# Routed rows kept as planes of 16-bit halves and loaded by a transposing DMA, with eight result buffers and new instruction orders

## What is computed

```python
h = _layernorm(x) * (1 + ca) + sa
x = x + ga * attn(h)      # h + 0.5 * (mamba forward + mamba backward), 16 states, 512 inner channels
h = _layernorm(x) * (1 + cb) + sb
x = x + gb * ffn(h)       # routed experts plus a shared expert
```

```python
scores = softmax(xt @ gate_w.T); top_vals, idx = top_k(scores, 2)
xs = xt[:, None, :] * weights[:, :, None]
for e in range(8):
    h  = silu(xs @ w1[e].T + b1[e])
    x2 = h @ w2[e].T + b2[e]
    x3 = xs @ w3[e].T + b3[e]
    y  = y + sum(x2 * x3 * mask)
z = (silu(xt @ sw1.T) * (xt @ sw2.T)) @ sw3.T
return y + z
```

## Time and profile before

| | |
|---|---|
| median of 3 runs | 2058.6 us |
| the profiled execution's own time | 2058.04 us |
| its span | 2056.2 us |
| mean granted TensorE clock | 0.922 |
| busy: TensorE, VectorE, ScalarE, GpSimd | 88%, 94%, 78%, 87% |

### The profile page before, as it was taken

One profiled execution on the slowest core, in us unless ns is written; L12 is line 12 of the kernel. 1 busy time (PEld: TensorE's weight loads), 2 busy tenths in 40 slices (PEclk: granted clock), 3 DMA queues, 4 the chain that ended last, 5 costly groups with the idle time before them and its releaser, 6 DMA issues.

```text
span 2056.2 us, 25386 instructions
## 1 busy us (share of the span) xinstructions
PE 1813.9 (88%) x6768; PEld 829.7 (40%) x6768; DVE 1925.5 (94%) x1820; ACT 1599.3 (78%) x3362; POOL 1798.3 (87%) x612
## 2 busy tenths in 40 slices
PE   7788898979898979788898889898977799999997
PEld 3333333424242423232323233332322256569996
DVE  7999999999999999999999999999999998857776
ACT  5886779898989898877788898989896844546664
POOL 5689999999999999999999999999999953545555
PEclk9999898989898989898989989898987899999999
DMA  7736454544545353535362635354545334635555
GB/s 268 244 117 152 105 138 110 134 108 121 124 116 125 109 133 105 124 106 143 85 164 72 157 92 141 100 131 115 131 97 146 112 126 140 253 135 91 94 94 76
DMA packets 140653, 263.93 MB, mean 128 GB/s; under 512 B 21840, under 2 KB 44368, under 8 KB 139488
## 3 DMA queue, kind: packets, MB, share of 16 engines
q1 hardware_dynamic: 125920, 240.58, 43.3%
q0 software_dynamic: 13296, 17.80, 5.0%
q10 hardware_dynamic: 1296, 3.93, 0.5%
HBM read 193.10 MB, written 70.19 MB: 128 GB/s over the span
## 4 chain that ended last, share of the span: by engine, by line
PE 27%; ACT 23%; DVE 22%; issue 16%; POOL 11%; DMA 1%; DVEq 0%; ACTq 0%; POOLq 0%; SPq 0%
DVE hst L1935 13%; ACT psum L1399 9%; POOL hst L1058 7%; DVE dbu L1914 5%; PE psum L2739 4%; PE psum L2495 3%; PE psum L2925 3%; ACT dbu L1431 3%; PE psum L2934 3%; PE psum L2945 3%; PE psum L2753 2%; POOL dbu L1046 2%; PE psum L2415 2%; ACT sp_tmp L1368 1%; ACT dt L1363 1%
## 5 line engine op out<-in xcount | busy, mean ns | idle before, releaser
L1058 POOL TENSOR_TENSOR hst<-hst,c_rep 128x2048 f32<-128x2048 f32 x254 | 1146.8, 4548 | 3.5 <-ACT state L1385 3.4
L1399 ACT ACTIVATE psum<-dt_rep,neg_a 128x512 f32<-128x512 f32 (+1 forms) x1024 | 659.8, 676 | 123.1 <-DVE hst L1935 118.5
L1935 DVE TENSOR_TENSOR_SCAN hst<-psum,state,dbu 128x1024 f32<-128x1024 f32 x264 | 603.8, 2325 | 0.5 <-DVE score L2012 0.4
L1935 DVE TENSOR_TENSOR_SCAN hst<-psum,dbu 128x1024 f32<-128x1024 f32 x248 | 554.6, 2269 | 6.9 <-ACT psum L1399 6.8
L1914 DVE TENSOR_TENSOR dbu<-psum,b_rep 128x2048 f32<-128x2048 f32 x177 | 400.2, 2261 | 6.6 <-PE psum L2480 6.5
L1046 POOL TENSOR_TENSOR dbu<-dtu_rep,b_rep 128x2048 f32<-128x2048 f32 x79 | 360.1, 4559 | 12.4 <-DVE hst L1935 7.4
L2480 PE MATMUL psum<-dt,same 32*128 32x512 f32 x354 | 217.5, 696 | 103.0 <-DVE dbu L1914 94.9
L2495 PE MATMUL psum<-hst,same 128*32 128x512 f32 x2048 | 267.3, 669 | 43.2 <-POOL hst L1058 43.2
L2427 PE MATMUL psum<-xp,taps 128*128 128x512 f32 x512 | 237.1, 606 | 5.4 <-ACT sp_tmp L1365 5.3
L1189 POOL DMA_INDIRECT out_x<-h,target_u x71 | 110.8, 1560 | 107.1 <-issue 51.7
L1431 ACT ACTIVATE dbu<-first_decay,dbu,state 128x1 f32<-128x1 f32 x504 | 160.0, 376 | 20.5 <-DVE dbu L1914 18.9
(11 more groups left out here) (246 smaller groups left out, 2623.9 us busy)
## 6 DMA issues: line engine op xcount, KB each, us to landing
dt_rep<-dt_scratch SPq DMA_DIRECT2D x256, 256.0 KB, 4.8
dtu_rep<-dtu_scratch SPq DMA_DIRECT2D x316, 64.0 KB, 1.9
taps<-taps_scratch SPq DMA_DIRECT2D x64, 256.0 KB, 4.5
b_rep<-bc_scratch SPq DMA_DIRECT2D x64, 256.0 KB, 4.9
c_rep<-bc_scratch SPq DMA_DIRECT2D x64, 256.0 KB, 7.7
dt_scratch<-dt SPq DMA_DIRECT2D x48, 256.0 KB, 6.2
h<-slot_scratch SPq DMA_DIRECT2D x71, 129.5 KB, 2.3
sp_tmp<-t_scratch SPq DMA_DIRECT2D x16, 512.0 KB, 6.9
```

The source lines that it names most:

```text
L1058: nc.gpsimd.tensor_tensor(h, h, c_rep[q % 2][:], ALU.mult).then_inc(prod_done, 1)
L1399: nc.scalar.activation(psum[:, PS_A + i, kept], dt_rep[:, G % 2, j, kept], ACT.Exp, scale=neg_a[:, q % 2, u, i:i + 1]).then_inc(exp_done, 1)
L1935: nc.vector.tensor_tensor_scan(both(hst[:, U % RING, groups, :]), both(psum[:, PS_A + 2 * pair:PS_A + 2 * pair + 2, :]), both(dbu[:, U % D ...
```

## The change

- A routed row is stored in HBM as two planes of 16-bit halves: the 256 low halves of its float32 values, then the 256 high halves, then number and flags, padded to 1088 bytes. ScalarE scales into a new tile `weighed` first, and one more activation copy for each send (2048 elements of 16 bits a partition) parts the halves into `send`.
- In the tile loop SP issues a transposing DMA of 128 rows by 512 halves into `turned_halves` (4 buffers) and a second small DMA of number and flags into `xt_meta` (8 buffers). `turn_tile` is gone from TensorE. `join_halves` on ScalarE takes the place of `copy_tile`: 512 elements of 16 bits from SBUF instead of 256 float32 from PSUM, two tiles ahead instead of one, into 4 buffers.
- The load of tile s+4 waits for `join_halves(s)`, and for the tile s-4 to have been gated.
- The result `yt` has 8 buffers, so `bias_result(s)` waits for the DMA of tile s-8.
- The order lists of TensorE, VectorE and ScalarE behind the scan are new.

```diff
-ROW = DM + 1 + BATCH
+META = 1 + BATCH
+ROW = DM + 16
...
-        target_u = sb3("target_u", [P, IDS], U32)
+        target_u = sb3("target_u", [P, 16], U32)
...
-        yt = part(8, 4, 1)
-        xtT = part(12, 2, 1)
+        yt = part(4, 8, 1)
+        xtT = part(12, 4, 1)
+        xtT_halves = xtT.bitcast(U16).rearrange("p n (d b) -> p n d b", b=2)
...
+        turned_halves = part(18, 4, 1).bitcast(U16).rearrange("p n (b d) -> p n b d", b=2)
+        xt_meta = flat[:, 22 * DM:22 * DM + 8 * META].rearrange("p (n d) -> p n d", n=8)
...
+        weighed = sb3("weighed", [P, NT, DM])
+        weighed_halves = weighed[:].bitcast(U16).rearrange("p t (d b) -> p t b d", b=2)
...
             def load_tile(s):
...
-                sp.dma_start(xt[:, s % 4, :], slot_dram[bass.ds(rows[s], P)]).then_inc(xt_loaded[s % 4], 16)
+                nc.sync.dma_start_transpose(turned_halves[:, s % 4].rearrange("p b (k c) -> p (b k) c", k=KD),
+                                            slot_halves[bass.ds(rows[s], P), 0:2 * DM]).then_inc(xt_loaded[s % 4], 16)
+                sp.dma_start(xt_meta[:, s % 8, :], slot_dram[bass.ds(rows[s], P), DM:DM + META]
+                             ).then_inc(xt_loaded[s % 4], 16)
...
             for s in range(TILES - 4):
-                sp.wait_ge(target_kept, s + 1)
-                sp.wait_ge(gate_done, s + 1)
+                sp.wait_ge(xtT_copied, s + 1)
+                if s >= 4:
+                    sp.wait_ge(target_kept, s - 3)
+                    sp.wait_ge(gate_done, s - 3)
...
                 for tt in range(NT):
                     t = n * NT + tt
-                    nc.scalar.activation(send[:, m % 4, tt, 0:DM], normed(p, tt), ACT.Copy, scale=weight[:, k, t:t + 1]
+                    nc.scalar.activation(weighed[:, tt, :], normed(p, tt), ACT.Copy, scale=weight[:, k, t:t + 1]
...
+                act.wait_ge(scaled, (NT + 3) * m + NT + 2)
+                nc.scalar.activation(send_halves[:, m % 4], weighed_halves, ACT.Copy).then_inc(scaled, 1)
...
-            def copy_tile(s):
-                act.wait_ge(xt_turned, s + 1)
-                if s >= 2:
-                    act.wait_ge(hx_full, s - 1)
-                nc.scalar.activation(xtT[:, s % 2, :], psum[:, s % 2, 0:DM], ACT.Copy).then_inc(xtT_copied, 1)
+            def join_halves(s):
+                act.wait_ge(xt_loaded[s % 4], 32 * (s // 4 + 1))
+                if s >= 4:
+                    act.wait_ge(hx_full, s - 3)
+                nc.scalar.activation(xtT_halves[:, s % 4], turned_halves[:, s % 4].rearrange("p b d -> p d b"), ACT.Copy
+                                     ).then_inc(xtT_copied, 1)
...
             for s in range(TILES):
                 silu_tile(s)
-                if s + 1 < TILES:
-                    copy_tile(s + 1)
+                if s + 2 < TILES:
+                    join_halves(s + 2)
...
             def bias_result(s):
                 dve.wait_ge(y_full, s + 1)
-                if s >= 4:
-                    dve.wait_ge(y_stored[s % 4], 16 * (s // 4 + 1))
+                if s >= 8:
+                    dve.wait_ge(y_stored[s % 4], 16 * (s // 4))
...
-            def turn_tile(s):
-                pe.wait_ge(xt_loaded[s % 4], 16 * (s // 4 + 1))
-                if s >= 2:
-                    pe.wait_ge(xtT_copied, s - 1)
-                for k in range(KD):
-                    ins = nc.tensor.transpose(psum[:, s % 2, k * P:(k + 1) * P], xt[:, s % 4, k * P:(k + 1) * P], ident[:])
-                ins.then_inc(xt_turned, 1)
```

Of the new orders, the ends of the lists matter most. On TensorE `count_places(7)` moves up past `out_second(6)` and `shared_part(1, 7, False)`:

```diff
             shared_part(0, 7, False)
             out_end(6)
+            count_places(7)
             out_second(6)
             shared_part(1, 7, False)
-            count_places(7)
             shared_part(0, 7, True)
+            shared_part(2, 7, False)
             shared_part(1, 7, True)
-            shared_part(2, 7, False)
             shared_part(3, 7, False)
```

and on ScalarE the last sends lie between other shared parts:

```diff
             exp_scores(7)
+            scale_tokens(6, 0)
+            scale_tokens(6, 1)
             silu_shared(0, 7)
+            scale_tokens(7, 0)
             silu_shared(1, 7)
-            scale_tokens(7, 0)
+            silu_shared(2, 7)
             scale_tokens(7, 1)
-            silu_shared(2, 7)
             silu_shared(3, 7)
```

More of the change, by code:

```diff
@@ L398, in mixer_and_experts @@
         w1 = sb3("w1", [P, 2, KD, DM])
+        weighed = sb3("weighed", [P, NT, DM])
+        weighed_halves = weighed[:].bitcast(U16).rearrange("p t (d b) -> p t b d", b=2)
+        send_words = send[:].bitcast(U32)
+        send_halves = send[:].bitcast(U16)[:, :, :, 0:2 * DM].rearrange("p m t (b d) -> p m t b d", b=2)
         ffn.close()
@@ L1732, in scale_tokens @@
                     act.wait_ge(trash_kept, 48)
+                if m >= 1:
+                    act.wait_ge(scaled, (NT + 3) * m)
                 if m >= 4:
@@ L1746, in _ @@
             copy_out(STEPS - 1, 0)
-            exp_scores(1)
+            silu_shared(1, 2)
+            scale_tokens(0, 0)
             copy_out(STEPS - 1, 1)
-            silu_shared(1, 2)
             silu_shared(2, 2)
+            scale_tokens(0, 1)
+            turned(3)
             copy_logits(2)
             silu_shared(3, 2)
-            scale_tokens(0, 0)
-            scale_tokens(0, 1)
+            silu_shared(0, 3)
             exp_scores(2)
-            turned(3)
-            silu_shared(0, 3)
             scale_tokens(1, 0)
@@ L1762, in _ @@
             silu_shared(2, 3)
-            exp_scores(3)
             turned(4)
             silu_shared(3, 3)
+            exp_scores(3)
+            silu_shared(0, 4)
             scale_tokens(2, 0)
-            silu_shared(0, 4)
+            silu_shared(1, 4)
             copy_logits(4)
-            silu_shared(1, 4)
             scale_tokens(2, 1)
@@ L1772, in _ @@
             silu_shared(2, 4)
+            turned(5)
+            silu_shared(3, 4)
             scale_tokens(3, 0)
-            silu_shared(3, 4)
-            turned(5)
+            scale_tokens(3, 1)
             silu_shared(0, 5)
+            copy_logits(5)
+            scale_tokens(4, 0)
             silu_shared(1, 5)
-            scale_tokens(3, 1)
-            copy_logits(5)
             exp_scores(5)
@@ L1842, in _ @@
                 rows_landed(act, m)
-            copy_tile(0)
+            join_halves(0)
+            join_halves(1)
             begin_gate(0)
@@ L2228, in _ @@
             gate_y(STEPS - 1, NC - 1)
-            add_shared(1, 1)
             dve.wait_ge(f_const, F_CONST)
             rank_experts(0)
+            add_shared(1, 1)
             modulate_early(0)
             place_tokens(0)
+            add_mixed(3)
             shared(0, 2)
+            norm_statistics(3)
             rank_experts(1)
-            add_mixed(3)
+            norm_begin(3)
             shared(1, 2)
+            norm_end(3)
+            shared(2, 2)
             place_tokens(1)
-            norm_statistics(3)
-            shared(2, 2)
-            norm_begin(3)
+            add_mixed(4)
+            add_mixed(5)
             shared(3, 2)
-            norm_end(3)
             shift_logits(2)
-            add_mixed(4)
+            norm_statistics(4)
             rank_experts(2)
@@ L2248, in _ @@
             add_shared(2, 1)
-            norm_statistics(4)
+            norm_begin(4)
             place_tokens(2)
-            norm_begin(4)
+            norm_end(4)
             shared(0, 3)
-            norm_end(4)
+            shared(1, 3)
+            add_mixed(6)
             shift_logits(3)
-            shared(1, 3)
             shared(2, 3)
+            shared(3, 3)
             rank_experts(3)
-            shared(3, 3)
-            add_mixed(5)
+            norm_statistics(5)
             place_tokens(3)
-            norm_statistics(5)
             add_shared(3, 0)
+            norm_statistics(6)
             add_shared(3, 1)
             norm_begin(5)
+            shift_logits(4)
+            shared(0, 4)
             norm_end(5)
-            shared(0, 4)
-            shift_logits(4)
+            norm_begin(6)
             shared(1, 4)
-            add_mixed(6)
+            rank_experts(4)
             shared(2, 4)
-            rank_experts(4)
-            norm_statistics(6)
+            place_tokens(4)
             shared(3, 4)
-            place_tokens(4)
-            norm_begin(6)
+            add_mixed(7)
+            norm_statistics(7)
             add_shared(4, 0)
-            add_mixed(7)
             add_shared(4, 1)
@@ L2850, in _ @@
             shared_part(3, 4, False)
+            turn(5)
             shared_part(2, 4, True)
-            turn(5)
             shared_part(3, 4, True)
+            shared_part(0, 5, False)
+            count_places(4)
+            shared_part(1, 5, False)
             out_begin(4)
-            count_places(4)
-            shared_part(0, 5, False)
-            shared_part(1, 5, False)
+            router(5)
             out_end(4)
-            router(5)
             out_second(4)
```

133 lines of the change are left out of this document (65 added, 68 removed).

## The result

The changed kernel takes 2062.6 us (median of 20 runs, 2057.9 to 2066.6) against 2058.7 for the kernel before (20 runs, 2057.2 to 2061.8): a ratio of 1.0016, 95% interval 1.0009 to 1.0022. That is slower by 3 to 4 us, at the edge of the 0.2% that the forecast called no change, and not the 10 us faster that it gave. The profiled execution has a span of 2061.2 us.

What follows compares the result with a forecast made beforehand. TensorE was taken to bound the tile loop, VectorE the scan, which the change leaves alone. -15.6 + 4 + 0.5 + 1 = -10.1 us gave 2047.9 against the profiled 2058.0, or 2048.5 as median; range 2042 to 2082.

Steps and rivals of the forecast that it cites:

- TensorE's part: Tile loop: without its transposes TensorE takes 2.62 us a tile, 0.22 less over 71 tiles, 15.6 us off the path.
- GpSimd term: Tile loop: GpSimd, waiting for its sends to land, lags after each expert change; 4 us stay over at the end.
- signs named for a right forecast: Tile loop: line 2925 every 2.62 us, GpSimd's lag up to 6 us by the end, no VectorE wait on sends.
- Rival 1: Tile loop: results land later and eat the gain, about 2058 us; chance 0.17 together with the shared-stage stall rival.
- the forecast's formula: GpSimd's time in the tile loop is 187.6 + 39 dL, so each 0.1 us on a landing costs 3.9 us.
- Rival 2: Tile loop: transposing loads crowd the DMA engines, at most 2.0 us a tile, landings 0.8 longer: 2077 us; chance 0.25.
- Rival 3: Tile loop: a transposing load's four blocks go in series, 7.6 us a tile, 338 us more, 2396; chance 0.04.
- Rival 4: Shared stage: stalls of 10 us give the gain back, about 2058 us; chance 0.17 together with the late-landing rival.
- The terms of +0.5 and +1 us: +0.5 for the longer sends in the shared stage; +1 at the seam for the first transposing load and join.
- At half speed: ScalarE in the tile loop: alternating-plane copy at half speed adds another 0.43 us, 2.61 a tile, still within 2.62.

Runs made afterwards that it cites:

- experiment 6: Changed kernel with GpSimd's waits written as constants for these inputs, so no register is loaded, two sends in flight: 2055.6 us, ratio 0.9982.
- experiment 9: Kernel before the change, with constant waits and three accumulating sends in flight: 2057.6 us, ratio 0.9995.
- experiment 8: Changed kernel with constant waits and three accumulating sends in flight instead of two: 2044.2 us, ratio 0.9924.
- experiment 5: Changed kernel with only a bound (runtime check) added on the register values that GpSimd waits against: 2071.2 us, ratio 1.0057.
- experiment 1: Kernel before, TensorE's transposes left out, plain loads kept, a bound on GpSimd's register values; products of unturned rows: 2068.2 us, ratio 1.0040.
- experiment 2: Changed kernel with the transposing DMA replaced by a plain one of the same bytes, and a bound on GpSimd's register values: 2070.1 us, ratio 1.0052.
- experiment 7: Changed kernel with constant waits and the transposing DMA replaced by a plain one of the same bytes: 2053.6 us, ratio 0.9971.

## Why the prediction was wrong

**TensorE's part was right.** The period is 2.62 us, ScalarE and VectorE stay below it, and with the sends out of the way the kernel takes 2044.2 us. The sum without its GpSimd term, 2058.6 - 15.6 + 1.5, was 2044.5.

**The step that failed is the term of +4 us for GpSimd and the landing of its results.** The mechanism, its place and the pattern of pairs were named; its size is 18.4 us (2062.6 - 2044.2). Two parts of it were measured; taken from the ratios and their intervals they are 7 and 12 us, give or take 2 and 3:

- 7.0 us are register loads (6 against the changed kernel). They did not stand in the forecast at all. In the kernel before they are hidden, as TensorE's 2.84 us a tile leave GpSimd time, and experiment 9 changes nothing. The trace of before had them, as steps of 3.5 to 4 us without a change of expert, and they were overlooked.
- 11.4 us are the two sends in flight (8 against 6). The traces have 11.1 of them between the first send and the last: 183.4 us in experiment 8, which is 70 steps of 2.62, and 194.5 in experiment 6. There the eight changes take 41.1 us (5.1 each, against the 4.7 of the forecast) and the other 62 steps 2.47 us each (against 2.42). The two differences are 3.5 and 3.4 us, and with the 4 that were counted that is 10.9.

The 4.65 us for a change was one of the shortest of its kind: in the trace of before the eight changes take from 4.44 to 6.28 us, 39.6 in all. So 2.0 of the 3.5 us could have been read there, and 1.5 are new. The pair of 4.83 us was not a short one. Pairs right behind a change and without a load take 4.54 to 4.84 us before, and the eight of experiment 6 have a mean of 4.82. What is longer are later steps, such as one of 4.36 us into tile 13, where GpSimd has to work off its lag and in the kernel before had none. In experiment 6 a send starts 2.2 us or more behind the end of VectorE's result from tile 7 on, and 15 us at the end; in experiment 8 it is back at 0.8 us behind each change but the last.

Two of the signs named for a right forecast did not come: the lag at the end is 17 us in the changed kernel and not 6, and VectorE waits 6.1 us for the sends.

**Rival 1 came about in time, and partly in cause.** It said that the landings would lengthen under new DMA work, with even at 0.32 us a landing. They did, by 0.2 to 0.3 us: the median is 3.8 us in the kernel before and in experiment 9, and 4.0 to 4.1 in the changed kernel and in experiments 5, 6 and 8. By the forecast's formula 0.2 us would cost 8. But where the median is 3.9, in experiments 1 and 2, the time is only 3.0 and 1.1 us below that of experiment 5. The transposing DMA is some 2.0 us of the 18.4, not clear of the scatter (7 against 6). The greater part was there before any load was changed (experiment 1).

**Rival 2** (crowding, 2077 us) and its upper bound of 2.0 us a tile on the engines fell: the loads take 0.79 us a tile with the small DMA. **Rival 3** fell: from the issue at 1839.58 to the join of the first tile at 1842.97 are 3.39 us for all four blocks, close to the 3.5 taken. The Trainium skill's page DMA: Bandwidth & Descriptors, section Latency and other measured facts, has 261 GB/s for a transposing DMA. Here the plain load's 0.50 us on the engines and the 0.16 of experiment 7 make an estimate of 0.66 us for 128 KB, some 200 GB/s, slower than the page but of its order. **Rival 4** (stalls in the shared stage) would have been real without the new orders: they are worth 4.8 to 7 us. With them the stage was 0.3 us longer, from 1652.69 to 1840.45 against 1650.62 to 1838.11, and the seam behind it 0.7 us longer, 3.26 against 2.58. The terms of +0.5 and +1 us held.

**A slip without effect.** At half speed the copy of halves would have cost 512 x 0.93 = 0.48 us more, not 0.43, and ScalarE would have had 2.66 us a tile, just over the 2.62. The copy takes 685 ns, 0.30 us over the old one, so it did not come to that.

**The buffers.** The forecast said that eight buffers would hide the lag and that with four it would reach TensorE. With eight TensorE still waits 2.8 us in the changed kernel, and no longer once the register loads are gone (experiment 6). With four, and constant waits, it waits 8.7 us, yet that costs only 1.9 us, not clear of the scatter.

**How the loads' 7.0 us divide.** They are loaded ahead of tiles 1, 8, 16, 24 and so on to 64. Right behind a change of expert, at tiles 8 and 40, the step is 2.0 and 2.1 us against 1.9 in experiment 6: there the loads are nearly free. The pairs that end with tiles 16, 24, 32, 48, 56 and 64 have a mean of 5.93 us against 4.93, so 1.0 us each. The step into tile 1 is 2.3 us longer, part of which the next tiles make good.

**Still open:** why the landings are longer in the changed kernel also with plain loads (4.0 us in experiment 7), and why GpSimd's later pairs take longer than those right behind a change.

## What to carry to other kernels

When a cut takes the bound close to a second chain, price that chain by the mean of all its steps, its odd ones too (here register loads every eighth tile), and not by one row of each kind; 0.1 us a step was 7 us. Look for what sets the depth of that chain: one more send in flight, with its waits freed of the loads, was worth nothing clear of the scatter in the kernel before, and it turned a change that gained nothing into one that gains 13 to 16 us. And an experiment that adds so much as a bound on a register value needs a run with that alone beside it.

## What the runs showed of the hardware

- A transposing DMA of 128 rows by 512 halves holds SP's queue for 1.20 us, and the small DMA behind it for 0.41, as SP's timeline of experiment 8 shows:

```profile
1839.79 1.20 SPq L952 DMA_TRANSPOSE h<-slot_scratch  x1
1841.20 0.41 SPq L954 DMA_DIRECT2D h<-slot_scratch  x1
1841.74 1.20 SPq L952 DMA_TRANSPOSE h<-slot_scratch  x1
```

  Both together, 1.95 us from one load to the next, fit into 2.62 us with little to spare.
- Loading eight register values on GpSimd made the step to tile 16 take 4.0 us, and 5.9 with the check of their bound. The pair of steps that ends there takes 7.7 us with loads and check, 6.1 with loads and 5.1 with neither. Right behind a change of expert the loads without the check cost 0.1 to 0.3 us.
- With two accumulating sends in flight GpSimd starts a pair of them every 4.8 to 4.9 us (experiment 6). With three it starts one every 1.86 us (experiment 8), 1.55 of its own time and 0.30 of issue. A send that waits for the one just before it starts 4.4 to 6.3 us behind that one (the kernel before, experiments 6 and 8), with a mean of 5.0.
- A copy of 512 two-byte elements out of two planes takes ScalarE 685 ns, 10% more than 512 float32 (623), and one of 2048 takes 1.91 us: no half speed.
